# Stage weights read from HBM one block earlier, during the normalisation, in a one-core audio-tower kernel

## The reference

```python
h = _L0_tok_ref(x, L0_tok_W, L0_tok_b)
h = h + _L0_attn_ref(_layernorm(h), ...)   # two-layer bidirectional Mamba
h = h + _L0_ffn_ref(_layernorm(h), ...)    # 64 experts, 8 of a grouped top-k
h = h + _L1_attn_ref(_layernorm(h), ...)   # Mamba-2, two directions
h = h + _L1_ffn_ref(_layernorm(h), ...)    # 16 relu experts, top 4
h = h + _L2_attn_ref(_layernorm(h), ...)   # attention, 8 heads
h = h + _L2_ffn_ref(_layernorm(h), ...)    # 8 relu experts, top 1
h = h + _L3_attn_ref(_layernorm(h), ...)   # gated linear attention
h = h + _L3_ffn_ref(_layernorm(h), ...)    # 8 gated experts, top 2
return h
```

## Time and profile before

| | |
|---|---|
| median of 3 runs | 3247.32 us (3238.9 to 3250.64) |
| the profiled execution, own time | 3243.43 us |
| its span, first to last instruction | 3241.6 us |
| PE busy | 2544.6 us, 78% of the span |
| DVE busy | 2352.4 us, 73% |
| POOL, ACT busy | 1419.5 us, 1327.5 us |
| DMA | 203.35 MB, 62 GB/s over the span |

### The profile page before, as it was taken

The page is one execution under the profiler, slowest core; times in us unless marked ns, Lnnn a source line. Parts: engine busy times, 40 slices in busy tenths (PEclk is TensorE's granted clock), DMA queues, the critical chain, the costliest instruction groups (busy, mean ns, idle before and its releaser), DMA issues. The chain is left out here.

```text
span 3241.6 us, 29207 instructions
## 1 busy us (share of the span) xinstructions
PE 2544.6 (78%) x8955; PEld 1510.7 (47%) x8955; DVE 2352.4 (73%) x3437; ACT 1327.5 (41%) x2109; POOL 1419.5 (44%) x897
## 2 busy tenths in 40 slices
PE   1778777677787772999857979479999659969599
PEld 0323222332332331666534837357777437733366
DVE  5699799759988976555557485658888548859566
ACT  2644444254454431222253343147776326730222
POOL 1499789649978971111123516110000310017266
PEclk9899889889999985999878989779999859979799
DMA  5155065116505410565300000022120011100021
GB/s 138 34 121 115 13 131 111 36 23 127 118 23 119 105 54 17 134 139 139 92 17 10 17 0 0 5 74 76 62 79 27 6 53 63 43 12 18 12 81 65
DMA packets 86604, 203.35 MB, mean 63 GB/s; under 512 B 12816, under 2 KB 25184, under 8 KB 77920
## 3 DMA queue, kind: packets, MB, share of 16 engines
q1 hardware_dynamic: 85952, 200.63, 24.6%
q0 software_dynamic: 512, 1.05, 0.1%
HBM read 198.76 MB, written 2.88 MB: 62 GB/s over the span
## 5 line engine op out<-in xcount | busy, mean ns | idle before, releaser
L532 DVE TENSOR_TENSOR m1x_HS<-m1x_R,m1x_HS 128x512 fp32r<-128x512 f32 x256 | 175.8, 691 | 69.2 <-ACT m1x_HS L500 64.9
L493 ACT ACTIVATE m1x_R<-m1x_ph,m1s_W 128x512 f32<-128x512 f32 x256 | 176.3, 689 | 107.2 <-PE m1x_ph L308 106.5
L1337 POOL TENSOR_TENSOR t2x_KM<-t2x_KT,t2x_HM 128x2048 f32<-128x2048 f32 x8 | 28.8, 3603 | 432.7 <-ACT t2x_KT L1410 416.0
L1688 POOL TENSOR_TENSOR t3xs_QH<-t3xs_HS,t3xa_Q 128x512 f32<-128x512 f32 x64 | 81.0, 1266 | 287.9 <-DVE t3xs_HS L1672 287.9
L829 DVE TENSOR_TENSOR m0x_T<-m0x_S,m0x_pb 128x512 f32<-128x512 f32 x128 | 88.1, 689 | 131.3 <-PE m0x_pb L308 131.2
L815 ACT ACTIVATE m0x_S<-m0x_pa 128x512 f32<-128x512 f32 x128 | 76.5, 598 | 214.2 <-PE m0x_pa L308 214.2
L2117 PE MATMUL t0x1fs_acc<-t0x1fs_HC,g_ident 128*128 128x512 f32 x256 | 133.6, 654 | 38.6 <-POOL t0x1fs_HC L2198 38.5
L2117 PE MATMUL t0x0fs_acc<-t0x0fs_HC,g_ident 128*128 128x512 f32 x256 | 133.2, 651 | 38.3 <-POOL t0x0fs_HC L2198 38.2
L2117 PE MATMUL t0x1bs_acc<-t0x1bs_HC,g_ident 128*128 128x512 f32 x256 | 131.2, 641 | 39.3 <-POOL t0x1bs_HC L2198 39.2
L2117 PE MATMUL t0x0bs_acc<-t0x0bs_HC,g_ident 128*128 128x512 f32 x256 | 130.2, 639 | 35.7 <-POOL t0x0bs_HC L2198 35.6
L2198 POOL TENSOR_TENSOR t0x1bs_HC<-t0x1bs_HS,t0x1bs_CB 128x1024 f32<-128x1024 f32 x64 | 149.1, 2360 | 10.7 <-DMA t0x1bs_CB<-t0x1b_bc_rows 4.2
(11 more groups left out here) (915 smaller groups left out, 7637.6 us busy)
## 6 DMA issues: line engine op xcount, KB each, us to landing
m0x_GS<-m_gate_rows SPq DMA_DIRECT2D x64, 512.0 KB, 6.6
t0x0fs_CB<-t0x0f_bc_rows SPq DMA_DIRECT2D x32, 512.0 KB, 6.3
t0x0bs_CB<-t0x0b_bc_rows SPq DMA_DIRECT2D x32, 512.0 KB, 6.5
t0x1fs_CB<-t0x1f_bc_rows SPq DMA_DIRECT2D x32, 512.0 KB, 6.4
t0x1bs_CB<-t0x1b_bc_rows SPq DMA_DIRECT2D x32, 512.0 KB, 6.6
m1x_GS<-m_gate_rows SPq DMA_DIRECT2D x16, 1024.0 KB, 4.7
m1s_W<-in_L_w SPq DMA_DIRECT2D x16, 514.0 KB, 3.3
m2x_GS<-m_gate_rows SPq DMA_DIRECT2D x8, 1024.0 KB, 4.7
```

Source lines behind the costliest of these rows:

```text
L493: a.activation(R[:, s % 4, :], ph[s % 4][:, :], ACT.Relu, bias=W[:, e % RAW, weights.cut + c:weights.cut + c + 1]).then_inc(relu_ready, 1)
L532: v.tensor_tensor(HS[:, s % 4, 1, :], R[:, s % 4, :], HS[:, s % 4, 0, :].bitcast(F32), ALU.subtract).then_inc(low_made, 1)
L1337: nc.gpsimd.tensor_tensor(KM[:, i % 2, :, :], keys, spread(HM[:, :], W), ALU.mult).then_inc(km_made, 1)
L1688: nc.gpsimd.tensor_tensor(QH[:, s % 4, :], HS[:, s % 4, :], Q[:, c], ALU.mult).then_inc(read, 1)
```

## The change

A helper `Ahead` collects pairs of tile and source. `normalise` gets it and issues its DMAs on SP at the start of its own block. The tiles are allocated in the stage around both blocks. The readers in the next block wait on `fetched.loaded`, which counts the collected DMAs. It is applied in seven places (all layers but t0). In the routers the first expert weights are started there too (`fetched.more`). In t1 the four DMAs of the projection move, the other eight stay. In t3 all seven move and are waited for together. Core of the diff:

```diff
+class Ahead:
+    def __init__(self, st):
+        self.st, self.loads, self.more = st, [], None
+        self.loaded = st.sem("fetched_loaded")
+    def tile(self, name, shape, *sources):
+        t = self.st.sb(name, shape)
+        for part, source in sources:
+            self.loads.append((t[part], source))
+        return t
+    def issue(self, sp):
+        for tile, source in self.loads:
+            sp.dma_start(tile, source).then_inc(self.loaded, 16)
+        if self.more is not None:
+            self.more(sp)
+    def all(self):
+        return 16 * len(self.loads)
...
@@ normalise
         with nc.Block() as block:
+            @block.sync
+            def _(sp):
+                if fetched is not None:
+                    fetched.issue(sp)
+
             @block.vector
...
@@ route_softmax (route_grouped alike)
-                sp.dma_start(wr[:, :], w_router[:, :]).then_inc(loaded, 16)
-                sp.dma_start(br[:, :], b_router.partition_broadcast(P)).then_inc(loaded, 16)
-                weights.start_loads(sp)
                 for g in range(GROUPS):
                     sp.wait_ge(turned_read, g + 1)
...
-                pe.wait_ge(loaded, 32)
+                pe.wait_ge(fetched.loaded, fetched.all())
...
@@ attend
-            @block.sync
-            def _(sp):
-                for tile, src in ((WK, wk), (WQ, wq), (WV, wv), (WO, wo), (HM, head_mask), (LM, lane_mask)):
-                    sp.dma_start(tile[:, :], src).then_inc(loaded, 16)
-                sp.dma_start(GB[:, 0, :], gamma.partition_broadcast(P)).then_inc(loaded, 16)
-                sp.dma_start(GB[:, 1, :], beta.partition_broadcast(P)).then_inc(loaded, 16)
-                sp.wait_ge(loaded, 128)
...
-                pe.wait_ge(loaded, 128)
+                pe.wait_ge(fetched.loaded, fetched.all())
...
@@ gated_recurrence
-                        pe.wait_ge(mid_loaded, 48)
+                        pe.wait_ge(fetched.loaded, fetched.all())
...
-                        pe.wait_ge(loaded, 64)
...
@@ mamba2_layer
-            normalise(nc, name + "n", H, XT, ident, XN)
+            fetched = Ahead(sp_)
+            WP = fetched.tile("WP", [P, 256], (ALL, w["pre_w"]))
...
+            normalise(nc, name + "n", H, XT, ident, XN, fetched=fetched)
...
-                    sp.dma_start(WP[:, :], w["pre_w"]).then_inc(loaded, 16)
-                    sp.dma_start(PB[:, :], w["pre_b"].partition_broadcast(P)).then_inc(loaded, 16)
-                    sp.dma_start(GB[:, 0, :], w["pre_ln_g"].partition_broadcast(P)).then_inc(loaded, 16)
-                    sp.dma_start(GB[:, 1, :], w["pre_ln_b"].partition_broadcast(P)).then_inc(loaded, 16)
                     sp.dma_start(cc["blocks"][:, :], consts["c_blocks"]).then_inc(loaded, 16)
                     sp.dma_start(cc["own"][:, :], consts["c_own"]).then_inc(loaded, 16)
                     load_front(sp, front, w, 0)
-                    sp.wait_ge(loaded, 96)
+                    sp.wait_ge(loaded, 32)
...
-                    pe.wait_ge(loaded, 96)
+                    pe.wait_ge(fetched.loaded, fetched.all())
...
@@ build, relu_layer
-            normalise(nc, name + "n", H, XT, ident)
...
+                fetched = Ahead(s)
+                router = router_tiles(fetched, ins[wr], ins[br], E)
+                fetched.more = weights.start_loads
+                normalise(nc, name + "n", H, XT, ident, fetched=fetched)
```

More of the change, by code:

```diff
@@ L241, in _ @@
                 dve.wait_ge(logits_ready, 1)
-                dve.wait_ge(loaded, 32)
+                dve.wait_ge(fetched.loaded, fetched.all())
                 link(nc.vector.tensor_tensor(logits[:, :, :], pl[:, :, :],
@@ L849, in _, with route_grouped @@
                     v.tensor_tensor(H[:, t, :], H[:, t, :], out[:, :].rearrange("p (t c) -> p t c", c=P), ALU.add)
-def route_grouped(nc, name, XT, XR, ident, iota, earlier, w_router, b_router, GT_rows, gate_rows, stored, weights):
+def route_grouped(nc, name, XT, XR, ident, iota, earlier, fetched, wr, br, GT_rows, gate_rows, stored, weights):
     E, NG, K, CAP = 64, 8, 8, 256
@@ L1442, in _ @@
                 v = nc.vector
-                dve.wait_ge(loaded, 128)
+                dve.wait_ge(fetched.loaded, fetched.all())
                 def values(i):
@@ L1585, in _ @@
                         v = nc.vector
-                        dve.wait_ge(mid_loaded, 48)
+                        dve.wait_ge(fetched.loaded, fetched.all())
                         v.tensor_scalar(B[:, 1:2], B[:, 0:1], -1.0, None, ALU.mult).then_inc(neg_made, 1)
@@ L2773, in _ @@
                 def _(dve):
-                    dve.wait_ge(loaded, 96)
+                    dve.wait_ge(fetched.loaded, fetched.all())
                     for g in range(GROUPS):
@@ L2888, in build @@
             weights = Weights(nc, s, ins["L0_units"], 4, 2 * P, 0)
-            route_grouped(nc, "m0r", XT, XR, ident, iota, consts["earlier"], ins["L0_ffn_gate_w"], ins["L0_ffn_gate_b"],
+            fetched = Ahead(s)
+            router = router_tiles(fetched, ins["L0_ffn_gate_w"], ins["L0_ffn_gate_b"], 64)
+            fetched.more = weights.start_loads
+            normalise(nc, "m0n", H, XT, ident, fetched=fetched)
+            route_grouped(nc, "m0r", XT, XR, ident, iota, consts["earlier"], fetched, *router,
                           GT_rows, gate_rows, stored, weights)
@@ L2904, in build @@
         recycle(nc)
-        normalise(nc, "t3n", H, XT, ident)
-        gated_recurrence(nc, "t3x", H, XT, ident, {n: ins["L3_attn_" + n] for n in
-                                                   ("Wq", "Wk", "Wg", "Wgk1", "Wgk2", "bgk2", "Wo", "units")})
+        with Stage(nc, "t3") as s:
+            w = {n[8:]: ap for n, ap in ins.items() if n.startswith("L3_attn_")}
+            fetched = Ahead(s)
+            tiles = [fetched.tile("W1", [P, 16], (ALL, w["Wgk1"])), fetched.tile("W2", [16, P], (ALL, w["Wgk2"])),
+                     fetched.tile("B", [P, 2], ((slice(None), slice(0, 1)), w["bgk2"]))]
+            tiles += [fetched.tile(n, [P, P], (ALL, w[n])) for n in ("Wk", "Wq", "Wo", "Wg")]
+            normalise(nc, "t3n", H, XT, ident, fetched=fetched)
+            gated_recurrence(nc, "t3x", H, XT, ident, w, fetched, *tiles)
         recycle(nc)
-        normalise(nc, "m3n", H, XT, ident)
         with Stage(nc, "m3s") as s:
@@ L2915, in build @@
             weights = Weights(nc, s, ins["L3_units"], 4, 2 * P, 3)
-            route_softmax(nc, "m3r", XT, XR, ident, iota, ins["L3_ffn_router_w"], ins["L3_ffn_router_b"], 8, 2,
+            fetched = Ahead(s)
+            router = router_tiles(fetched, ins["L3_ffn_router_w"], ins["L3_ffn_router_b"], 8)
+            fetched.more = weights.start_loads
+            normalise(nc, "m3n", H, XT, ident, fetched=fetched)
+            route_softmax(nc, "m3r", XT, XR, ident, iota, fetched, *router, 8, 2,
                           gateF, gate_rows, stored, weights, quick_bias)
```

71 lines of the change are left out of this document (23 added, 48 removed).

## The result

The changed kernel took **3210.9 us** (median of 4, 3209.8 to 3213.6) against 3244.2 for the kernel before (median of 4, 3238.9 to 3250.6): ratio 0.9902, interval 0.9885 to 0.9919. Its profiled execution took 3213.63 us with a span of 3211.8, 29.8 less than before.

A forecast was written before the change was run, and what follows sets the result against it. Serial blocks between barriers, with PE waiting for DMAs behind seven normalisations, were taken as the bound. 3243.4 - 30.8 (waits) - 6 (clock) = 3206.6, plus half of 3.9 for a median: 3208.6 us, range 3197 to 3222.

The forecast's parts named there:

- The seven waits: Blocks behind seven normalisations: PE would start with the other engines instead of waiting for DMAs; 30.8 us gained in all.
- The loads land in time: Normalisation's 10.4 us cover the longest load list, t2's 6.9 us, with some 3.5 us to spare.
- early expert weights: Routers: POOL splits them only behind its own subtraction, well after they land, so earlier arrival gives 0.
- SP's branches: SP's new branches in eight blocks cost 0, as SP has 10 us there.
- Is POOL or ACT late next?: Routers and t1: with PE earlier, POOL would not end the block last at m3 or t1; no cost.
- What the early transfers collide with: Normalisations: DMA transfers now beside PE's weight loads and DVE were taken to cost 0.
- The clock: PE's granted clock at t1, t2, t3, m2, m3: a shorter gap saves 8.5 us, cut to 6; ends -3 and 14.
- three signs: Clock gain shown by t2's first projections at 0.99, and m2's and m3's routers each under 7.0 us.
- rival B: Waits go, clock gives nothing or PE crosses barriers up to 0.9 us later: 3214.6 us, late crossing 3221; chance 0.33.
- A: The forecast: waits go and the clock gives some; 3208.6 us, between 3197 and 3212; chance 0.58.
- C: Half the effect: another engine becomes last in the routers, 3229 us, or loads don't run ahead, 3245; chance 0.07.
- D: Slower: m1's expert block drops from clock 0.98 to 0.85, costing 58 us; 3272 us; chance 0.02.

The follow-up runs named there:

- run 2: Kernel before with only attention's (t2's) eight loads issued early, in the normalisation; 3235.8 us against 3242.7, ratio 0.9974.
- run 8: Changed kernel with the loads of t1, t2 and t3 issued again in the block that reads them; 3228.7 us against 3242.9, ratio 0.9958.
- run 3: Changed kernel with the expert weights started in the router's block again; 3210.1 us, ratio 0.9900.
- run 4: Changed kernel without DVE's cast of the chosen indices to fp32; 3213.4 us, ratio 0.9911.
- run 5: Changed kernel with POOL's subtraction in m1's and m2's routers waiting for DVE's gates; 3209.9 us, ratio 0.9901.
- run 10: Changed kernel with POOL's subtraction late in m1's and m2's routers and m3's third and fourth splits late too; 3205.0 us, ratio 0.9893.
- run 6: Changed kernel with three extra 512-column PE matmuls ahead of the transposes in each of the seven normalisations; 3209.7 us, ratio 0.9904.
- run 1: Changed kernel again with no edit, with a second trace; 3209.3 us, ratio 0.9901.
- run 7: Changed kernel with the expert bias rows of m1, m2 and m3 also loaded in the normalisation; 3202.3 us, ratio 0.9885.
- run 9: Changed kernel with bias rows early and POOL's subtraction late in m1's and m2's routers; 3204.1 us, ratio 0.9881.
- run 11: Changed kernel with the late subtraction (m1, m2), m3's late splits and the early bias rows together; 3201.5 us, ratio 0.9879.

## Why the prediction was right, and by how much it was off

- *The seven waits, 30.8 us.* Right in each place: PE starts with the others (0.02 us apart at m0), the DMA waits are gone, and of the bounds 0 and 0.9 us on the crossing 0 was the value. PE's starts came forward by 30.4 us. Runs 2 and 8 agree with the places adding up, as far as their noise allows.
- *The loads land in time; early expert weights worth 0; SP's branches 0.* Right: no wait for them is left, and run 3 puts the weights at nothing that can be measured.
- *"Is POOL or ACT late next?"*, answered *"Covered."* **This step failed.** It asked only whether POOL would end last, and POOL does not. What it left out is that POOL and DVE can hold each other up. Terms of 0 at m1, m2 and m3 measured 0.7, 1.1 and 1.25 us, 3.1 together; runs 4, 5 and 10 show the cause. "What the early transfers collide with" looked for such a thing in the wrong pair: DMA and DVE. The cast of 0.37 us at m3, beside the POOL operation that the step itself reads from the earlier trace rows, was the warning in the trace of before.
- *The clock, 6 of 8.5 us.* **Mis-sized**: some 2.3 us in the first trace. Against the wait of its place t1 got +0.9, t2 -1.2, t3 +2.3, m3 +1.7 (router 5.3 us for 7.0), m0, m1 and m2 within 0.2 of 0 once the stall is taken off, and the other blocks lost 1.2, which is put down to the clock here but was not followed block by block. Of the three signs that the prediction named for this term two failed: t2's first projections ran at 0.50 and m2's router took 7.0 us. What held is that the clock, once up, carries over the short gap: in every early-loaded place of all the traces but run 6's, the stage began at 2.4 GHz where the gap behind the transposes read 0.98 or 1.00, and at 1.2 GHz where it read 0.50. What failed is *where* it rises. The prediction took t2, m2 and m3 over from the trace of before; in the changed kernel it rose during the transposes of t3 and m3, in run 1 at m0 too. And run 2 shows that t2's 2.5 us were too much even where the rise came: 0.6.
- *The sum.* Forecast for the profiled execution 3206.6, measured 3213.6: 7.0 over, of which 3.1 are the stall, 3.7 the clock, and the rest rounding. By the same sum rival B, the waits and no clock, has 3212.6 for that execution and is nearer. The number thus doesn't speak for A over B: the clock's gain and the stall nearly cancel. It is the rows that show both. The medians came nearer, 3208.6 against 3210.9, and that is luck: 2 us had been added for a slower median, which in fact lay 2.7 below the profiled execution. As a difference the forecast was 38.7 us and the measured one 33.3, against a median before that had itself moved from 3247.3 to 3244.2 with a fourth run. The result lies in A's range, 2.3 above its number and 3.7 below B's. C and D are out: no router ends on POOL, and m1's experts took 376.5 us for 377.3.

## What to carry to other kernels

Where blocks are divided by a barrier, a DMA issued in the block that reads it costs the last issue plus its latency on the path: 3 to 7 us of PE's start each time here, back when it is issued a block earlier, and the gains of such places add up within the noise. Price it by where the other engines start, not by the wait that the profile gives: the bias rows' waits of 2.7 to 2.9 us moved PE's start by 1.3 to 1.5. When one engine's work moves forward and another's stays, look at which of their operations now overlap, even if neither is last; for DVE and POOL, list the two-input operations and casts that would fall beside a POOL operation.

## What was not expected of the hardware

**DVE held by POOL for the whole of POOL's operation.** A cast of 0.23 us took up to 1.51 (run 6), a 0.19 us operation 1.34 and 2.34, each until POOL's operation ended; DVE's index searches beside the same operation kept their 0.16 us. The Trainium skill says this: "SBUF — State Buffer", section "Who interferes with whom", tells of a pair of ports shared by the two engines that the first comer holds for its whole instruction. It says that a DVE instruction with two SBUF inputs contends there with a GpSimd instruction that reads SBUF, and that casts can. The rows agree, down to the operation that began 0.04 us too late and waited 2.34.

**The granted clock rises in other places from one execution to the next.** With the same instructions t3's gate matmuls ran in 3.6 us in the changed kernel and in runs 1, 3 and 5, in 5.6 to 5.9 in runs 4, 6, 7, 9, 10 and 11. The matmuls of m0's router took 7.1 us in the changed kernel and 5.0 in run 1, which is the same kernel. There PE had stood idle for 21.5 us before the transposes, and the clock rose to full during them (0.55 over their last 3.5 us, 1.00 in the gap behind). Nor is a high clock before a stage enough to keep it: run 6 brought 0.99 to the end of m0's transposes and the router ran at 0.50. What decides it is left open. Its size, 2 us in one place and the other sign in the next, is enough to hide edits worth 1 to 3 us, which showed in the block steps and not in the medians.
